# Normalisation moved back to VectorE in the output tiles, half a head moved into the chunk loop, and an early load dropped

## The chip, the cores and the metric

One Trainium2 chip, all 8 cores. Each core runs the same program on its own batch element; no core talks to another. The metric is device time in microseconds of the slowest core.

## The reference, cut to what matters

Per core, `x` is 2048 x 2048 float32 (`L` rows of `C` features). One layer joins a state-space branch `s` and a feed-forward branch `g`, both fed by the same layer-normed `xn`:

```python
xn = layernorm(x)                                  # mean m1, 1/std r1 per row
# s: a second layer norm, in_proj (C -> 96), conv of width 3, silu,
#    selective scan over 16 states -> y, then y @ out_proj_W.T + xn
s  = attn_ref(xn, ...)
# g: int8-like rows times ternary weights, w1, w3: 2048 -> 5632, w2: 5632 -> 2048
h  = silu(bitlinear(xn, w1)) * bitlinear(xn, w3)
g  = silu(bitlinear(h, w2))
return x + s * g
```

## The kernel before, in words

The program is a row of blocks. Inside a block each engine has its own in-order queue and they meet at semaphores; a block ends when all engines have ended it. Every `@blk.vector`, `@blk.scalar`, ... function appends to one engine's queue, so the order in which the Python code emits them is the order in which each engine runs them.

**`ph01`** (lines 380 to 702) works through `NE = 8` row blocks of 256 rows. For block `e`:

- `emit_xdma(e)` loads the rows into `xh2[e % 2]` from SP's queue. It waits until block `e - 2` has left the buffer.
- `emit_head(e)` (line 399): ScalarE computes mean and variance (L408 to L423, all small and large passes over the 2 row tiles); VectorE waits for them and normalises in place (L434, L437 x2), takes the row maximum (L444 x2) and makes the quantisation scales (L449 to L464). Then the scales are turned into a row and spread over the partitions: TensorE transposes (L474), VectorE copies (L483), SP sends two small transfers (L492), TensorE multiplies by ones (L500, L502), VectorE copies to `sxB` and `sxinvB` (L509, L511).
- `emit_chunks(e)` (line 516): ScalarE computes the statistics of the second norm (L525 to L540) once the head's scales are there. Then 16 chunks `cc`: TensorE transposes 128 columns (L562), VectorE copies them out (L574), TensorE multiplies them with the in-projection (L593), VectorE scales and casts them into `qx` (L583, L585).
- `emit_tail(e)` (line 602) spreads the second norm's factors in the same way (L613 to L671) and writes `xin` (L678 to L683).

The driver emits head(0), and then for each `e`: tail(e - 1), chunks(e), xdma(e + 2), head(e + 1), and from `e = 2` on two units of weight means (`emit_means`, POOL loads 1 MB, ScalarE sums it, L278).

**`attn`** (line 731) does the convolution and the scan. POOL builds a selection matrix `sel` (L734, L737) while VectorE makes two small operations for `nm1r1 = -m1 * r1` (L746, L748) and then starts the convolution (L750, L758, L762).

**`m13`** does the two big products with `w1` and `w3` and stores `h` to `h_scr` in device memory. **`hfin`** (line 1196) finds the row maxima of `h` and spreads the scales into `shB`. At its start POOL already loads the first two 512 KB tiles of `h` (L1202, `h_preload`).

**`m2_0` and `m2_1`** (line 1315) each compute half of the rows of `g`'s last product, in 11 slabs of 4 tiles `ht`. `emit_prep_early` loads `h` (L1360, POOL, each load waits for VectorE's product of two tiles earlier) and, in half 0, `w2T` (L1379, SP, 1 MB each, three buffers); VectorE scales `h` to integers (L1411), ScalarE copies to bfloat16 (L1429) and makes signs of the weights (L1448, L1451), VectorE adds them (L1475). `emit_m2_units` runs the matmuls (L1532) and VectorE adds each result to `f_half` (L1549, L1551).

Each half ends with 8 **output tiles** `tt` (lines 1573 to 1654), one per 128 rows:

- SP loads the tile of `x` (L1582), 1 MB, into `xre`. The load of tile `tt` is emitted behind the store of tile `tt - 1`, in one queue.
- TensorE computes `y @ out_proj` (L1601), four products of 512 columns, in turn into `ps_op` and the two `ps_f`, so each of them is free again two tiles later.
- ScalarE makes `silu` of `f_half` (L1612), and then normalises `xre` into `xnb` with `scale = r1`, `bias = nm1r1` (L1620).
- VectorE adds the product (L1632, or L1635 and L1638 as two halves), multiplies with the gate (L1641) and adds `xre` (L1643), and SP stores (L1651).

```python
sy.wait_ge(s_v.h, ob_hist.get(tt - 2, fwait[2 * tt + 1]))      # x load of tile tt, L1581
...
t.wait_ge(s_v.h, ob_hist[tt - 2])                              # matmul of tile tt, L1591
```

`ob_hist[tt]` is the semaphore value after L1643 of tile `tt`.

Of the kernel before, what the change touches and what calls it, by code (L numbers as in the profile page):

```python
# [15 lines left out]
C = 2048  # L16
# [31 lines left out]
def build_core_program(stop_after=None):  # L48
# [331 lines left out]
    with nc.Block("ph01") as blk:  # L380
# [18 lines left out]
        def emit_head(e):  # L399
# [68 lines left out]

            @blk.tensor
            def _(t):  # L470
                t.wait_ge(s_v.h, p4v_hist[e])
                if e >= 2:
                    t.wait_ge(s_v.h, bc2c_hist[e - 2])
                s_t.inc(t.transpose(ps_bc[0][0:2 * TPE, 0:128],  # L474
                                    xcol[:, sb1:sb1 + 2 * TPE], ident[:]))
# [40 lines left out]
        def emit_chunks(e):  # L516
# [31 lines left out]
            for cc in range(NCC):  # L548
                par = (2, 3, 0, 1)[cc % 4]
# [141 lines left out]
        emit_head(0)  # L691
        for e in range(NE):
            if e >= 1:
                emit_tail(e - 1)
            emit_chunks(e)
            if e + 2 < NE:
                emit_xdma(e + 2)
            if e + 1 < NE:
                emit_head(e + 1)
# [31 lines left out]
    with nc.Block("attn") as blk:  # L731
# [9 lines left out]
        nm1r1 = xcol[:, 3 * NTT:4 * NTT]  # L741
# [452 lines left out]
    h_preload = {}  # L1194

    with nc.Block("hfin") as blk:
        @blk.gpsimd
        def _(g):
# [110 lines left out]
    sgs_all = {}  # L1309
    hq_last = {0: None, 1: None}  # L1310
    prev_store = [0, 0]
    for half in range(2):
        hq_sems = {}
        hm1_sems = {}
        with nc.Block(f"m2_{half}") as blk:
# [6 lines left out]
            def emit_prep_early(sbi):  # L1322
# [24 lines left out]
                def _(g):  # L1347
                    for k in range(sbn):
                        ht = base + k
                        par = ht % 2  # L1350
                        if half == 0 and ht < 2:
                            hlds[k] = h_preload[ht]
                            continue
# [13 lines left out]
                if half == 0:  # L1367
                    for k in range(sbn):
                        sgs_all[base + k] = s_a.v + min(2, sbn) + k + 1
# [67 lines left out]
                if half == 0:  # L1437
# [3 lines left out]
                    def _(sc):  # L1441
                        for k in range(sbn):
# [13 lines left out]
                            assert sgs_all[ht] == got  # L1456
# [116 lines left out]
            for tt in range(TPH):  # L1573
# [14 lines left out]
                def _(t):  # L1588
                    t.wait_ge(s_v.h, fwait[2 * tt + 1])
                    if tt >= 2:  # L1590
                        t.wait_ge(s_v.h, ob_hist[tt - 2])  # L1591
                    if tt == 1:
                        t.wait_ge(s_v.h, f_ok)
                    inst = None
                    for j in range(4):
                        if tt % 2 == 0:
                            dst = ps_op[:, j * 512:(j + 1) * 512]
                        else:
                            dst = ps_f[j // 2][:, (j % 2) * 512:
                                               (j % 2 + 1) * 512]  # L1600
                        inst = t.matmul(dst,  # L1601
# [7 lines left out]
                def _(sc):  # L1609
                    sc.wait_ge(s_v.h, fwait[2 * tt + 1])  # L1610
                    sc.wait_ge(s_o[fp].h, st_hist.get(tt - 2, prev_store[fp]))
                    sc.activation(gbuf[:],  # L1612
                                  f_half[:, tt * C:(tt + 1) * C],
                                  AF.Silu, scale=hscol[:, gt:gt + 1])
                    sc.drain()
# [11 lines left out]
                def _(v):  # L1627
                    xnb = fscr1 if tt % 2 == 0 else sxinvB
                    v.wait_ge(s_t.h, opd)
                    v.wait_ge(s_a.h, gok)  # L1630
                    if tt % 2 == 0:
                        v.tensor_tensor(xnb[:], ps_op[:], xnb[:], ALU.add)  # L1632
                        v.drain()
                    else:
# [84 lines left out]
```

## Time and profile before

| | us |
|---|---|
| two timed runs | 3564.94 and 3662.07, median 3613.51 |
| profiled execution, its own time | 3567.97 |
| its span, slowest core (core 4) | 3566.3 |
| spans of the 8 cores | 3553.2 to 3566.3 |
| mean granted TensorE clock | 0.86 on every core |

The span runs from the first to the last instruction of core 4. Times of single instructions below are microseconds from its start. The profiled execution's own time is 1.7 us above its span; all terms below are set against that execution.

### The profile page before, as it was taken

To read this page: it belongs to the slowest core of one execution; us is meant where nothing else is said; L and a number is where in the kernel's file an instruction comes from. 1 tells how busy PE (TensorE), PEld (TensorE's weight loads), DVE (VectorE), ACT (ScalarE), POOL (GpSimd) and SP (SyncE) were. 2 spreads that over 40 slices of the span, in tenths; PEclk is the share of its full clock that TensorE was granted. 3 is DMA by queue.
4 is the path that set the end of the run, shared out by engine and by line. 5 is a ranking of instruction groups with operands and counts; after the bars stand their busy time and mean duration, and the time that the engine had idled before them with its cause. 6 is when DMAs were issued, how large, how long until landed. Compare 5 with 4: busy or idle time off the path is not lost. (4 is left out here: it accounts for less than half of the span.)

```text
span 3566.3 us, 29311 instructions; the slowest of 8 cores (3553.2 to 3566.3 us)
## 1 busy us (share of the span) xinstructions
PE 2501.6 (70%) x9525; PEld 1088.6 (31%) x9525; DVE 1844.2 (52%) x1799; ACT 1684.5 (47%) x1360; POOL 151.2 (4%) x283
## 2 busy tenths in 40 slices
PE   2454454996999999999999994355656733766772
PEld 1222221332444444444444442122222311323331
DVE  2545444884445554455445445445555534656653
ACT  3252514886666666666666661554453232111122
POOL 0000001110000000000000000000000000000000
PEclk9999996556999999999999996677778866888885
DMA  3112103996445454445454541554454234232213
GB/s 112 47 67 75 48 0 118 335 308 234 140 140 143 142 143 140 140 142 143 141 142 142 142 118 36 188 177 153 130 189 134 85 123 141 100 125 106 84 62 127
DMA packets 92611, 469.14 MB, mean 132 GB/s; under 512 B 12924, under 2 KB 13004, under 8 KB 58060
## 3 DMA queue, kind: packets, MB, share of 16 engines
q1 hardware_dynamic: 54412, 282.69, 25.1%
q0 software_dynamic: 38048, 184.57, 16.6%
q8 instruction: 78, 1.28, 0.2%
q14 instruction: 73, 0.60, 0.1%
HBM read 381.20 MB, written 85.98 MB: 131 GB/s over the span
## 5 line engine op out<-in xcount | busy, mean ns | idle before, releaser
L1532 PE MATMUL ps_f<-w2s,qhs 128*128 128x512 bf16 x2816 | 680.0, 407 | 425.4 <-DVE f_half L1551 261.9
L1071 PE MATMUL ps_a<-qx,w1q 128*128 128x512 bf16 x2816 | 632.2, 383 | 85.6 <-DVE hbuf L1116 73.7
L1079 PE MATMUL ps_b<-qx,w3q 128*128 128x512 bf16 x2816 | 622.1, 379 | 0.0
L1532 PEld LDWEIGHTS ps_f<-w2s,qhs 128*128 128x128 bf16 x2816 | 288.8, 103 | 818.0 <-issue 589.4
L1551 DVE TENSOR_TENSOR f_half<-f_half,ps_f 128x1024 f32<-128x1024 f32 x320 | 390.9, 1221 | 195.9 <-PE ps_f L1532 190.1
L1071 PEld LDWEIGHTS ps_a<-qx,w1q 128*128 128x128 bf16 x2816 | 275.1, 99 | 434.7 <-issue 118.5
L1079 PEld LDWEIGHTS ps_b<-qx,w3q 128*128 128x128 bf16 x2816 | 275.6, 98 | 332.2
L1429 ACT ACT_TABLE_LOAD x44 | 56.5, 1283 | 573.1 <-DVE fscr L1411 571.8
L1104 ACT ACT_TABLE_LOAD x88 | 112.9, 1283 | 447.5 <-DVE fscr L1095 447.5
L1411 DVE TENSOR_TENSOR fscr<-hbuf,shB 128x1024 int32<-128x1024 f32 x88 | 107.8, 1225 | 252.4 <-DMA hbuf<-h_scr 235.7
L1112 DVE TENSOR_TENSOR fscr<-ps_b,sxinvB 128x1024 f32<-128x1024 f32 x88 | 107.8, 1225 | 230.9 <-ACT fscr L1104 230.9
L593 PE MATMUL ps_ip<-xnTc,inprojT_sb 128*96 128x256 f32 x256 | 145.8, 672 | 107.9 <-DVE xnTc L574 107.9
L1042 DVE TENSOR_TENSOR w1q<-gscr 128x2048 bf16<-128x2048 bf16 x44 | 53.9, 1225 | 248.0 <-ACT gscr L1022 248.0
L1095 DVE TENSOR_TENSOR fscr<-ps_a,sxinvB 128x1024 f32<-128x1024 f32 x88 | 107.8, 1225 | 41.7 <-PE ps_b L1079 14.5
L887 PE MATMUL ps_sc<-bp_sb,sel 16*96 16x512 f32 x128 | 112.5, 1057 | 22.6 <-DVE y_sb L855 22.6
L525 ACT ACT_TABLE_LOAD x8 | 10.3, 1283 | 249.3 <-DVE xcol L464 249.3
L1051 DVE TENSOR_TENSOR w3q<-gscr 128x2048 bf16<-128x2048 bf16 x44 | 53.9, 1225 | 131.4 <-ACT gscr L1031 131.4
L1163 ACT ACT_TABLE_LOAD x88 | 112.9, 1283 | 11.4 <-issue 1.2
L1116 DVE SCALAR_TENSOR_TENSOR hbuf<-fscr,thrall 128x1024 f32<-128x1024 f32 x88 | 113.1, 1285 | 6.5
L574 DVE COPY xnTc<-ps_tr 128x256 f32<-128x256 f32 x128 | 54.4, 425 | 118.3 <-PE ps_tr L562 117.1
L908 PE MATMUL ps_cc<-cp_sb,sel 16*96 16x512 f32 x128 | 112.5, 1056 | 0.0
L1135 DVE SCALAR_TENSOR_TENSOR fscr<-hbuf 128x1024 f32<-128x1024 f32 x88 | 107.9, 1226 | 8.9 <-issue 0.2
(206 smaller groups left out, 2816.0 us busy)
## 6 DMA issues: line engine op xcount, KB each, us to landing
wstg<-w1L SPq DMA_DIRECT2D x44, 1024.0 KB, 11.6
wstg<-w3L SPq DMA_DIRECT2D x44, 1024.0 KB, 14.0
w2m<-w2T SPq DMA_DIRECT2D x88, 512.0 KB, 6.3
h_scr<-hbuf POOLq DMA_DIRECT2D x88, 512.0 KB, 4.2
hbuf<-h_scr POOLq DMA_DIRECT2D x88, 512.0 KB, 7.1
wstg<-w2T SPq DMA_DIRECT2D x30, 1024.0 KB, 9.4
wstg<-w1L POOLq DMA_DIRECT2D x22, 1024.0 KB, 7.6
wmst<-w1L POOLq DMA_DIRECT2D x22, 1024.0 KB, 9.6
```

The source lines that it names most:

```text
L593: inst = t.matmul(ps_ip[:], inprojT_sb[:, cc * D:(cc + 1) * D], xsl, start=(cc == 0), stop=(cc == NCC - 1))
L887: inst = t.matmul(ps_sc[0:D, j * 512:(j + 1) * 512], sel[:, n * D:(n + 1) * D], bp_sb[:, j * 512:(j + 1) * 512], start=True, stop=True)
L908: inst = t.matmul(ps_cc[0:D, j * 512:(j + 1) * 512], sel[:, n * D:(n + 1) * D], cp_sb[:, j * 512:(j + 1) * 512], start=True, stop=True)
L1071: t.matmul(ps_a[pu][:, j * 512:(j + 1) * 512], w1q[par][:, cc * 128:(cc + 1) * 128], qx[:, cc * L + th * HALF + j * 512: cc * L + th * HAL ...
L1079: inst = t.matmul(ps_b[pu][:, j * 512:(j + 1) * 512], w3q[par][:, cc * 128:(cc + 1) * 128], qx[:, cc * L + th * HALF + j * 512: cc * L + t ...
L1095: s_v.inc(v.tensor_tensor(fscr1[:, 0:HALF], ps_a[pu][:], sxinvB[:, th * HALF:(th + 1) * HALF], ALU.mult))
L1104: s_a.inc(sc.activation(fscr2[:, 0:HALF], fscr1[:, 0:HALF], AF.Silu, scale=thrall[:, 2:3]))
L1116: s_v.inc(v.scalar_tensor_tensor(hbuf[pu][:], fscr1[:, 0:HALF], thrall[:, 5:6], fscr2[:, 0:HALF], ALU.mult, ALU.mult))
L1135: v.scalar_tensor_tensor(fscr1[:, 0:HALF], hbuf[pu][:], -1.0, hbuf[pu][:], ALU.mult, ALU.max)
L1163: s_a.inc(sc.activation(w2m[wpar][:], w2m[wpar][:], AF.Abs, accum_out=mtmp[:, (2 + hf) * NH + ht: (2 + hf) * NH + ht + 1]))
L1532: inst = t.matmul(ps_f[pu][:, j * 512:(j + 1) * 512], qhs[sp][:, k * HALF + tt * 128: k * HALF + (tt + 1) * 128], w2s[sp][:, k * C + ch * ...
L1551: s_v.inc(v.tensor_tensor(dst, dst, ps_f[pu][:], ALU.add))
```

## The change

Three independent edits.

1. In `ph01` the head is cut in two. `emit_head_a` holds the load wait, ScalarE's statistics, and VectorE's normalisation up to the scales (L434 to L464). `emit_head_b` holds the transposition and spreading. `emit_chunks` gets a callback which emits `head_a(e + 1)` ahead of chunk 10 of block `e`; `head_b(e + 1)` stays where the head was.
2. In the output tiles the normalisation of `x` goes from ScalarE (L1620) to a `tensor_scalar` on VectorE, `nm1r1` and its two operations (L746, L748) go, and all tiles use `ps_op`, so that the matmuls of tile `tt` wait for VectorE's last operation of tile `tt - 1` instead of `tt - 2`.
3. The early load of the first two tiles of `h` (L1202) goes; they are loaded by `emit_prep_early` like the others.

```diff
-        def emit_head(e):
+        def emit_head_a(e):
...
             p4v_hist[e] = s_v.v
 
+        def emit_head_b(e):
+            sb1 = 3 * NTT + (e % 2) * 8
+
             @blk.tensor
...
-        def emit_chunks(e):
+        def emit_chunks(e, mid_cb=None):
...
             for cc in range(NCC):
+                if cc == 10 and mid_cb is not None:
+                    mid_cb()
...
         for e in range(NE):
             if e >= 1:
                 emit_tail(e - 1)
-            emit_chunks(e)
+            cb = (lambda e=e: emit_head_a(e + 1)) if e + 1 < NE else None
+            emit_chunks(e, cb)
             if e + 2 < NE:
                 emit_xdma(e + 2)
             if e + 1 < NE:
-                emit_head(e + 1)
+                emit_head_b(e + 1)
...
-            v.tensor_tensor(nm1r1, m1c[:], r1c[:], ALU.mult)
-            v.drain()
-            v.tensor_single_scalar(nm1r1, nm1r1, -1.0, ALU.mult)
-            v.drain()
...
-            for ht in range(2):
-                par = ht % 2
-                g.wait_ge(s_hd[par].h, hstore_total[par])
-                s_hd[par].inc(g.dma_start(
-                    out=hbuf[par][:],
-                    in_=dr["h_scr"][ht * 128:(ht + 1) * 128, 0:HALF]), 16)
-                h_preload[ht] = s_hd[par].v
...
                     t.wait_ge(s_v.h, fwait[2 * tt + 1])
-                    if tt >= 2:
-                        t.wait_ge(s_v.h, ob_hist[tt - 2])
-                    if tt == 1:
-                        t.wait_ge(s_v.h, f_ok)
+                    if tt >= 1:
+                        t.wait_ge(s_v.h, ob_hist[tt - 1])
...
-                    xnb = fscr1 if tt % 2 == 0 else sxinvB
-                    sc.wait_ge(s_x.h, xld)
-                    if tt >= 2:
-                        sc.wait_ge(s_v.h, ob_hist[tt - 2])
-                    s_a.inc(sc.activation(xnb[:], xre[:], AF.Identity,
-                                          scale=r1c[:, gt:gt + 1],
-                                          bias=nm1r1[:, gt:gt + 1]))
...
+                    v.wait_ge(s_x.h, xld)
                     v.wait_ge(s_t.h, opd)
                     v.wait_ge(s_a.h, gok)
...
+                    v.tensor_scalar(fscr1[:], xre[:], m1c[:, gt:gt + 1],
+                                    r1c[:, gt:gt + 1], ALU.subtract, ALU.mult)
+                    v.drain()
+                    v.tensor_tensor(fscr1[:], ps_op[:], fscr1[:], ALU.add)
+                    v.drain()
+                    v.tensor_tensor(fscr2[:], fscr1[:], gbuf[:], ALU.mult)
```

VectorE's queue before, from the end of chunk 15 of a block into the head of the next:

```order
L585 CAST qx<-fscr 128x256
L429 UNCONDITIONAL_BRANCH
L434 RECIPROCAL r1c<-sq 128x2
L437 TENSOR_SCALAR xh_0<-xh_0,m1c,r1c 128x2048 x2
L444 TENSOR_REDUCE stat<-xh_0 128x1 x2
...
L464 COPY xcol<-xcol 128x2
L478 UNCONDITIONAL_BRANCH
L483 COPY rowbuf<-ps_bc 4x128
```

The same engine after the change, from the end of chunk 9 on (lines shifted by 5: L590 is the old L585, L579 the old L574, L486 the old L483):

```order
L590 CAST qx<-fscr 128x256
L429 UNCONDITIONAL_BRANCH
L434 RECIPROCAL r1c<-sq 128x2
L437 TENSOR_SCALAR xh_0<-xh_0,m1c,r1c 128x2048 x2
L444 TENSOR_REDUCE stat<-xh_0 128x1 x2
...
L464 COPY xcol<-xcol 128x2
L574 UNCONDITIONAL_BRANCH
L579 COPY xnTc<-ps_tr 128x256
...
L590 CAST qx<-fscr 128x256
L481 UNCONDITIONAL_BRANCH
L486 COPY rowbuf<-ps_bc 4x128
```

The normalisation now stands between chunks 9 and 10, and the copy of the transposed scales follows chunk 15 directly. ScalarE's queue keeps its order.

VectorE's queue in two output tiles before:

```order
L1632 TENSOR_TENSOR fscr<-ps_op,fscr 128x2048
L1641 TENSOR_TENSOR fscr<-fscr,wstg 128x2048
L1643 TENSOR_TENSOR wstg<-fscr,wstg 128x2048
L1626 UNCONDITIONAL_BRANCH
L1635 TENSOR_TENSOR sxinvB<-ps_f,sxinvB 128x1024
L1638 TENSOR_TENSOR sxinvB<-ps_f,sxinvB 128x1024
L1641 TENSOR_TENSOR fscr<-sxinvB,wstg 128x2048
L1643 TENSOR_TENSOR wstg<-fscr,wstg 128x2048
```

and in one output tile after (every tile is alike):

```order
L1597 TENSOR_SCALAR fscr<-wstg,m1c,r1c 128x2048
L1600 TENSOR_TENSOR fscr<-ps_op,fscr 128x2048
L1602 TENSOR_TENSOR fscr<-fscr,wstg 128x2048
L1604 TENSOR_TENSOR wstg<-fscr,wstg 128x2048
```

One operation has come to VectorE, and the two half additions of the odd tiles have become one.

## Rows read from the trace of the kernel before

**Rows 1.** The page, part 1: busy time, share of the span, instructions.

```profile
PE 2501.6 (70%) x9525; PEld 1088.6 (31%) x9525; DVE 1844.2 (52%) x1799; ACT 1684.5 (47%) x1360; POOL 151.2 (4%) x283
```

**Rows 2.** Busy time by stretch: m2_0's slabs, its output tiles, m2_1's output tiles.

```profile
2227.00:2841.00 614.00, 358.02 (x1418) 149.33 (x1419) 323.34 (x265) 273.64 (x170) 22.18 (x42) 0.76 0.47 151
2841.00:2967.00 126.00, 39.97 (x55) 15.25 (x53) 55.17 (x28) 34.36 (x19) 0.00 (x0) 0.60 0.33 117
...
3436.00:3566.00 130.00, 39.21 (x54) 14.66 (x52) 54.85 (x28) 34.36 (x19) 0.00 (x0) 0.61 0.34 121
```

**Rows 3.** Timeline of ph01: start, duration, engine, line, operation, idle before.

```profile
250.25 0.42 DVE L574 COPY xnTc<-ps_tr 128x256 f32<-128x256 f32 x1 [0.16 <-issue]
...
255.63 0.39 ACT L423 ACTIVATE sq<-ssum,cns 128x2 f32<-128x2 f32 x1
...
284.71 0.42 DVE L574 COPY xnTc<-ps_tr 128x256 f32<-128x256 f32 x1 [1.00 <-PE ps_tr L562]
...
285.72 0.29 DVE L585 CAST qx<-fscr 128x256 bf16<-128x256 int32 x1
286.25 0.17 DVE L434 RECIPROCAL r1c<-sq 128x2 f32<-128x2 f32 x1 [0.23 <-issue]
...
295.27 0.17 DVE L464 COPY xcol<-xcol 128x2 f32<-128x2 f32 x1
...
296.24 0.28 DVE L483 COPY rowbuf<-ps_bc 4x128 f32<-4x128 f32 x1 [0.80 <-PE ps_bc L474]
```

**Rows 4.** Timeline of the start of attn.

```profile
539.87 1.48 POOL L734 IOTA sel<- 16x1536 f32 x1 [154.84 <-SPq L731]
...
540.21 1.17 DVE L748 TENSOR_SCALAR xcol<-xcol 128x16 f32<-128x16 f32 x1
541.46 5.22 DVE L750 TENSOR_SCALAR ucv<-xin,convw_sb,convb_sb 96x2048 f32<-96x2048 f32 x1
541.51 4.09 POOL L737 TENSOR_SCALAR sel<-sel 16x1536 f32<-16x1536 f32 x1 [0.17 <-issue]
```

**Rows 5.** Timeline of the output tiles of m2_0, and two rows of m2_1's.

```profile
2862.17 2.29 DVE L1643 TENSOR_TENSOR wstg<-fscr,wstg 128x2048 f32<-128x2048 f32 x1
...
2864.96 0.39 SPq L1582 DMA_DIRECT2D wstg<-x  x1
...
2871.99 2.09 ACT L1620 ACTIVATE fscr<-wstg,xcol,r1c 128x2048 f32<-128x2048 f32 x1 [11.42 <-DMA wstg<-x]
2874.19 2.29 DVE L1632 TENSOR_TENSOR fscr<-ps_op,fscr 128x2048 f32<-128x2048 f32 x1 [9.73 <-ACT fscr L1620]
...
2878.92 2.29 DVE L1643 TENSOR_TENSOR wstg<-fscr,wstg 128x2048 f32<-128x2048 f32 x1
...
2895.94 2.29 DVE L1643 TENSOR_TENSOR wstg<-fscr,wstg 128x2048 f32<-128x2048 f32 x1
...
3528.51 6.93 PE L1601 MATMUL ps_f<-outprojT_sb,y_sb 96*128 96x512 f32 x8 [10.08 <-DVE wstg L1643]
```

**Rows 6.** The line L437 in all of the trace: count, ns min/median/max.

```profile
L437 DVE TENSOR_SCALAR xh<-xh,m1c,r1c x16: 1345/1346/1348, 51.6 to 471.3; 128x2048 f32<-128x2048 f32 x16
```

**Rows 7.** Timeline of the start of m2_0.

```profile
2227.28 1.23 DVE L1411 TENSOR_TENSOR fscr<-hbuf,shB 128x1024 int32<-128x1024 f32 x1 [0.52 <-PEq L1196]
...
2241.47 1.22 DVE L1411 TENSOR_TENSOR fscr<-hbuf,shB 128x1024 int32<-128x1024 f32 x1 [11.58 <-DMA hbuf<-h_scr]
...
2245.36 1.23 DVE L1411 TENSOR_TENSOR fscr<-hbuf,shB 128x1024 int32<-128x1024 f32 x1 [2.67 <-DMA hbuf<-h_scr]
...
2256.92 2.00 ACT L1448 ACTIVATE wstg<-wstg,thrall 128x2048 bf16<-128x2048 f32 x1 [4.78 <-DMA wstg<-w2T]
...
2264.80 5.54 PE L1532 MATMUL ps_f<-w2s,qhs 128*128 128x512 bf16 x16 [40.44 <-DVE fscr L1411]
```

**Rows 8.** Timeline of the start of m2_1.

```profile
2967.32 1.04 POOL L1360 DMA_DIRECT2D hbuf<-h_scr  x2 [211.59 <-POOLq L1315]
...
2983.28 1.22 DVE L1411 TENSOR_TENSOR fscr<-hbuf,shB 128x1024 int32<-128x1024 f32 x1 [3.96 <-DMA hbuf<-h_scr]
```

More of the change, by code:

```diff
@@ L690, in build_core_program @@
         emit_xdma(1)
-        emit_head(0)
+        emit_head_a(0)
+        emit_head_b(0)
         for e in range(NE):
@@ L739, in build_core_program @@
         sel_ok = s_g.v
-        nm1r1 = xcol[:, 3 * NTT:4 * NTT]
         @blk.vector
@@ L1192, in build_core_program @@
     ps_f = [PS4(f"ps_f{i}", (128, HALF)) for i in range(2)]
-    h_preload = {}
     with nc.Block("hfin") as blk:
-        @blk.gpsimd
-        def _(g):
-            for ht in range(2):
-                par = ht % 2
-                g.wait_ge(s_hd[par].h, hstore_total[par])
-                s_hd[par].inc(g.dma_start(
-                    out=hbuf[par][:],
-                    in_=dr["h_scr"][ht * 128:(ht + 1) * 128, 0:HALF]), 16)
-                h_preload[ht] = s_hd[par].v
         thrw2 = finalize_mean(blk, (2 * NH, 4 * NH), 6, ps_op,
@@ L1308, in build_core_program @@
     wq_sems = {}
-    sgs_all = {}
     hq_last = {0: None, 1: None}
@@ L1350, in _ @@
                         par = ht % 2
-                        if half == 0 and ht < 2:
-                            hlds[k] = h_preload[ht]
-                            continue
                         if ht >= 2:
@@ L1365, in _ @@
                         hlds[k] = s_hd[par].v
-                if half == 0:
-                    for k in range(sbn):
-                        sgs_all[base + k] = s_a.v + min(2, sbn) + k + 1
                 wlds = {}
@@ L1455, in _ @@
                             sgs[k] = got
-                            assert sgs_all[ht] == got
                 if sbn > 2:
@@ L1589, in _ @@
                     t.wait_ge(s_v.h, fwait[2 * tt + 1])
-                    if tt >= 2:
-                        t.wait_ge(s_v.h, ob_hist[tt - 2])
-                    if tt == 1:
-                        t.wait_ge(s_v.h, f_ok)
+                    if tt >= 1:
+                        t.wait_ge(s_v.h, ob_hist[tt - 1])
                     inst = None
                     for j in range(4):
[L1596 to L1601, printed above, removed]
+                        inst = t.matmul(ps_op[:, j * 512:(j + 1) * 512],
                                         y_sb[:, gt * 128:(gt + 1) * 128],
@@ L1611, in _ @@
                     sc.wait_ge(s_o[fp].h, st_hist.get(tt - 2, prev_store[fp]))
[L1612 to L1615, printed above, removed]
-                    xnb = fscr1 if tt % 2 == 0 else sxinvB
-                    sc.wait_ge(s_x.h, xld)
-                    if tt >= 2:
-                        sc.wait_ge(s_v.h, ob_hist[tt - 2])
-                    s_a.inc(sc.activation(xnb[:], xre[:], AF.Identity,
-                                          scale=r1c[:, gt:gt + 1],
-                                          bias=nm1r1[:, gt:gt + 1]))
+                    s_a.inc(sc.activation(gbuf[:],
+                                          f_half[:, tt * C:(tt + 1) * C],
+                                          AF.Silu, scale=hscol[:, gt:gt + 1]))
                     sc.drain()
@@ L1627, in _ @@
                 def _(v):
-                    xnb = fscr1 if tt % 2 == 0 else sxinvB
+                    v.wait_ge(s_x.h, xld)
                     v.wait_ge(s_t.h, opd)
                     v.wait_ge(s_a.h, gok)
[L1631 to L1634, printed above, removed]
-                        v.tensor_tensor(xnb[:, 0:1024], ps_f[0][:],
-                                        xnb[:, 0:1024], ALU.add)
-                        v.drain()
-                        v.tensor_tensor(xnb[:, 1024:2048], ps_f[1][:],
-                                        xnb[:, 1024:2048], ALU.add)
-                        v.drain()
-                    v.tensor_tensor(fscr2[:], xnb[:], gbuf[:], ALU.mult)
+                    v.tensor_scalar(fscr1[:], xre[:], m1c[:, gt:gt + 1],
[4 more added lines that the diff above has]
+                    v.tensor_tensor(fscr2[:], fscr1[:], gbuf[:], ALU.mult)
                     v.drain()
```

## The prediction

> **What bounds the kernel now.** I read the page first: TensorE is busy for 70% of the span, VectorE for 52%, ScalarE for 47% [rows 1]. No engine is the bound of the whole, so each edit has to be priced in its own stage. Next I read the stretches. In the output tiles of either half TensorE is busy for 40 of 126 us and 39 of 130, VectorE for 55, ScalarE for 34, and the DMA engines at a third [rows 2]: nothing is full there, it is a chain. In the slabs of the first half no engine is full either (358, 323 and 274 of 614 us) [rows 2]. Then I followed the timeline at each of the four places that the diff touches. The large products of m13 (two thirds of TensorE's work) are not touched, nor is anything that they wait for.
>
> The chain of one output tile: VectorE's last operation of tile tt-1 ends at 2864.46 (2862.17 plus 2.29). SP issues the store and then the x load, at 2864.96. ScalarE has idled for 11.42 us when the load lets it start at 2871.99, 7.53 us after 2864.46. VectorE waits for ScalarE and starts at 2874.19, and three operations later it ends at 2881.21 (2878.92 plus 2.29) [rows 5]. So an even tile takes 16.75 us: 7.53 for store issue and load, 2.20 for ScalarE's pass with its handover, 7.02 for VectorE. The next, odd tile ends at 2898.23 (2895.94 plus 2.29), 17.02 us later, since its addition comes in two halves [rows 5]. TensorE is not in this chain, although it too starts only when VectorE has ended.
>
> **Edit 2, output tiles.** ScalarE's pass (2.20 us with the handover) leaves the chain. In its place VectorE runs a TENSOR_SCALAR over 128 x 2048 float32 with two per-row numbers. That is the very shape of L437: 1.346 us, in all 16 cases within 2 ns [rows 6]; with a gap of 0.07, as between VectorE's other neighbours, 1.42. A tile takes 7.53 + 1.42 + 7.02 = 15.97 us. Even tiles save 0.78, odd ones 1.05. Per half, tiles 1, 3, 5, 7 save 4.2 and tiles 2, 4, 6 save 2.3. Tile 0 loses: its x was there long before, ScalarE's pass was done beside the slabs, and now 1.42 us stand behind the last matmul. Net 5.1 per half, **-10.2 us** for both.
>
> The added wait: TensorE now begins tile tt after VectorE's end of tile tt-1. Before, at that same moment it began tile tt+1. So the start of its work is where it was, and only its consumer comes sooner. The slowest of these groups of 8 matmuls took 6.93 us [rows 5]; the granted clock was 0.60 to 0.61 in these stretches [rows 2], so much of it ran at 1.2 GHz. From VectorE's end to TensorE's end are then about 0.05 + 6.93 = 7.0 us, with a handover of 0.2 it is 7.2, and the load needs 7.53. The load stays last, by 0.3 us. Cost nothing; if this cover goes, each microsecond that TensorE is late costs 14 us over the 14 tiles. Silu stays on ScalarE, has no load ahead of it any more and runs far ahead of VectorE. Nothing else is queued behind TensorE's wait.
>
> **Edit 2, start of attn.** The small operations L746 and L748 stood ahead of the convolution. L748 handles 16 columns and yet took 1.17 us: it began while POOL's IOTA ran and ended at 541.38, when IOTA ended (541.35). L750 took 5.22 us and ended at 546.68, about a microsecond behind POOL's L737 (541.51 plus 4.09 is 545.60) [rows 4]. I read this as VectorE standing still while POOL works. Without the two, L750 is the one that stands waiting when IOTA ends, as L748 did, and gets its turn in the 0.16 us gap before L737: it would end at 541.35 + 1.35 = 542.7, or **-4.0 us**. The other end is 0: L737 comes first and L750 ends at 546.7 as before. I take -4.0, since L748 shows that the waiting operation goes first.
>
> The Trainium skill says in its GPSIMD Engine Reference, section Specifications, that GpSimd's access to SBUF is shared with VectorE, with contention against VectorE's two-port operations. These rows agree with it. By that page L1597 meets no such contention in the output tiles, where POOL has no row.
>
> **Edit 1, the head.** A chunk has VectorE idle for 1.00 us before its copy L574, in every chunk. Before, from the end of chunk 15 (285.72 plus 0.29, 286.01) to L483 at 296.24 there were 10.23 us: 0.24 gap, 9.19 for L434 to L464, 0.80 for TensorE's transposition [rows 3]. After, the 9.19 stand between chunks 9 and 10. There TensorE has finished chunk 10's transposition long before, so that L574 follows with a 0.16 gap, as the first chunk of a block does at 250.25 [rows 3]: 0.24 + 9.19 + 0.16 in place of the 1.00. At the end the scales' transposition has nothing to wait for, and L483 follows after some 1.00. Sum 8.59 + 1.00 = 9.59 against 10.23: 0.64 saved per head, seven heads, **-4.5 us**. VectorE and TensorE take turns in the chunks, so the 9.19 us themselves are not hidden: they stop the chunks wherever they stand. Bounds: 0, and 0.80 + 0.24 of each head saved, 7.3. ScalarE's statistics for the moved part end at 256.02 in the block whose first copy is at 250.25 and whose chunk 10 comes ten chunks of some 2.3 us later (three VectorE operations of 1.3 us in all and the 1.00 idle), at 273 [rows 3]; they are there in time by 17 us. The x load behind them and SP's queue keep their places, and ScalarE's second statistics start earlier, which nobody waits for.
>
> **Edit 3, the early load.** Before, VectorE scaled the first two tiles of h at once (2227.28), and the fourth at 2245.36, 18.1 us into the block, with 4 MB asked of the DMA engines till then (two tiles of h and three of w2T) [rows 7]. Behind the fourth product stand the first weight sum and thereby a weight load, the signs that wait for it (2256.92) and the first matmul (2264.80) [rows 7]. Without the early load the same engines have 5 MB to move before the fourth product. In proportion that is 22.6 us in place of 18.1, **+4.5 us**. The other bound is from the second half, which starts cold: the second product began 16.0 us after the first issue [rows 8], here it began 1.4 us into the block, so at most +14.6. The lower bound is 0, should the weight loads be what the signs wait for. I take 4.5, from the nearest rows. The slabs behind are a chain too [rows 2], so I carry the delay through undiminished.
>
> The Trainium skill has in DMA: Bandwidth & Descriptors, section Queues, rings and completion order, that each DMA engine serves the queues it has work for in turn, packet by packet. By that the h loads would not stand behind three weight loads but take half the rate, and the sum would be that of the rival "hidden" below. The trace speaks against it: the third tile's load kept VectorE waiting 11.58 us [rows 7].
>
> **Sum.** -10.2 - 4.0 - 4.5 + 4.5 = -14.2 us. From the profiled execution's 3567.97 us that gives 3553.8, rounded 3554. The two timed runs are 3564.94 and 3662.07; the profiled execution agrees with the lower one, and the median of 3613.51 is only the mean of two unlike runs.
>
> **The rivals.**
>
> - *Given back.* The first two h loads cost their full 14.6 us, and L750 loses its turn to L737: -10.2 - 4.5 + 14.6 = -0.1, 3568 us. For it: the second half's start [rows 8]. Against it: there 4 MB of w2s stood beside the h loads, here 3.
> - *Hidden.* The h loads share the engines evenly with the weight loads and are off the chain: -18.7, 3549 us. Against it: the 11.58 us.
> - *VectorE's added operation is slow.* A TENSOR_SCALAR took 5.22 us once [rows 4]. If the 16 new ones did, each would cost 3.87 more than counted, 62 us: 3553.8 + 62 = 3616 us, slower than before. It decides from 2.24 us per operation on (14.2 / 16 = 0.89 above 1.35). Against it: POOL has no work in the output tiles [rows 2], and L437 never took more than 1.348.
> - *The moved head waits in the middle.* If ScalarE's statistics came late, VectorE would stop at chunk 9 with TensorE behind it. Their passes take some 11 us, seven heads: 77 us, 3631 us. Against it: the 17 us of slack.
> - *TensorE becomes last in the output tiles.* If its work ended 1 us later than I have it, 0.7 x 14 = 10 us go: 3564.
>
> **How the numbers follow.** Chances: forecast 0.60 (3554, own range 3544 to 3565), given back 0.17, hidden 0.09, TensorE last 0.07, slow operation 0.03, late head 0.01, and 0.03 for what I do not see. The range reaches from 3540 (the hidden case with edit 1 at its bound is 3546, less some noise) to 3616, the slow operation: the upper side is wide because one run of the same kernel lay 97 us above the other. A measurement of this kernel can tell about 2% (71 us) from no change. No case reaches -71 us; the late head and half of the unseen would be at +2%. Faster 0.02, same 0.95, slower 0.03.
>
> **What would show it.** In the output tiles: VectorE idle before the new operation about 7.5 us, released by the x load and not by TensorE; 1.35 us each; tiles 16.0 us apart. In ph01: 9.4 us without chunks between chunks 9 and 10, no wait for ScalarE there, each block 0.6 us shorter. In attn: L750's duration and the end of POOL's L737. In m2_0: the first matmul some 42 us after the block's start instead of 37.5. The prediction is wrong if the stretches in between (m13, the slabs) change their lengths, or if the added operation takes other than 1.35 us.

## The result and the profile after

| | before | after |
|---|---|---|
| median of the runs, us | 3577.54 (3564.94 to 3727.86, 32 runs) | 3598.38 (3582.9 to 3768.95, 33 runs) |
| ratio after to before, 95% interval | | 1.005 (1.0033 to 1.0067) |
| profiled execution, its own time, us | 3567.97 | 3592.93 |
| its span on the slowest core, us | 3566.3 | 3591.3 |
| granted clock of its cores | 0.860 to 0.864 | 0.859 to 0.867 |

Some executions of either kernel run at a lower granted clock on some of the cores and take up to 5% longer; the ratio compares the others. The changed kernel is slower by 0.5%, some 18 us (0.005 x 3577.54). That is inside the 2% of "no change" and inside the range, but the forecast was 14 us faster, and the interval excludes every gain: the sign of the sum was wrong. Part 1 of the page after, which answers to [rows 1]:

```profile
PE 2503.7 (70%) x9525; PEld 1090.1 (30%) x9525; DVE 1862.5 (52%) x1805; ACT 1651.6 (46%) x1344; POOL 152.0 (4%) x283
```

The page sees that work moved from ScalarE to VectorE (18 us more on DVE, 33 less on ACT) and little else. Where the time went is in the stages. For the table the same marks (the first and last instruction of a stage) were read on all 8 cores of a profiled execution; it gives the medians over the cores, in us. The row "tiles 1 to 7" runs from the start of VectorE's last operation of tile 0 to the first load of half 1 (some 3 us behind the last tile's), the row below it from there to the start of VectorE's last operation of the last tile. The last column is explained with the experiments.

| stage | before | after | difference | forecast | after, x load behind the tail |
|---|---|---|---|---|---|
| ph01: first L434 to POOL's IOTA | 488.5 | 512.1 | **+23.6** | -4.5 | 482.9 |
| start of attn: IOTA to the end of the convolution | 11.8 | 10.2 | -1.6 | -4.0 | 10.2 |
| scan | 293.1 | 292.8 | -0.3 | 0 | 292.3 |
| m13 | 1340.1 | 1338.0 | -2.1 | 0 | 1337.3 |
| end of m13 to the block m2_0 | 43.6 | 43.5 | -0.1 | 0 | 43.5 |
| m2_0, start to first matmul | 35.6 | 40.8 | +5.2 | +4.5 | 41.2 |
| slabs, to VectorE's last operation of tile 0 | 579.3 | 582.8 | +3.5 | +1.4 | 583.9 |
| tiles 1 to 7 of half 0 | 123.4 | 118.0 | -5.4 | -6.5 | 118.0 |
| from there to the end of half 1 | 591.2 | 585.6 | -5.6 | -5.1 | 587.2 |
| sum | | | **+17.2** | -14.2 | |

The sum of the differences is what the ratio says (+18). All stages but one came within 3 us of the forecast; ph01 missed by 28.

What TensorE waits for in ph01 and the start of attn, in the kernel after (the time waited in all, how often, the longest, in us):

```profile
PE ps_bc L503 <- DMA rows<-rowbuf: 53.5, 8, 8.8
...
PE ps_bc L664 <- DMA rows<-rowbuf: 22.5, 8, 2.9
```

And the same two lines of code in the kernel before:

```profile
PE ps_bc L500 <- DMA rows<-rowbuf: 22.6, 8, 2.9
PE ps_bc L659 <- DMA rows<-rowbuf: 22.5, 8, 2.9
```

`rows` is the pair of 1 KB transfers with which the head spreads the scales over the partitions. The tail's pair (L664, before L659) costs 2.8 us each time, before and after. The head's pair cost 2.8 each time before, and now costs 53.5 in all. Two of the eight heads have no x load near them; the other six take (53.5 - 2 x 2.8) / 6 = 8.0 us each. The timeline of one of them, after (start, duration, engine, line, operation, idle before with its releaser):

```profile
243.30 0.37 SPq L387 DMA_DIRECT2D xh<-x  x1
243.55 0.28 DVE L486 COPY rowbuf<-ps_bc 4x128 f32<-4x128 f32 x1 [0.79 <-PE ps_bc L477]
243.90 1.25 SPq L495 DMA_DIRECT2D rows<-rowbuf  x2
...
251.19 1.19 PE L503 MATMUL ps_bc<-rows,ones 1*128 1x256 f32 x2 [7.82 <-DMA rows<-rowbuf]
251.25 1.28 ACT L408 ACT_TABLE_LOAD   x1 [10.81 <-DMA xh<-x]
253.34 0.43 DVE L512 COPY sxB<-ps_bc 128x256 f32<-128x256 f32 x1 [9.51 <-PE ps_bc L505]
```

and one of the kernel before:

```profile
286.56 0.37 SPq L387 DMA_DIRECT2D xh<-x  x1
...
296.59 1.17 SPq L492 DMA_DIRECT2D rows<-rowbuf  x2
...
298.90 1.19 PE L500 MATMUL ps_bc<-rows,ones 1*128 1x256 f32 x2 [2.84 <-DMA rows<-rowbuf]
```

Before, SP issues the 2 MB x load at 286.56 and the small rows 10.0 us later; they land in 2.3 (296.59 to 298.90). After, SP issues the rows 0.6 us behind the load, and they land 7.3 us later, at 251.19, in the same moment as the load (ScalarE, which waits for it, goes on at 251.25). Over the six blocks and eight cores it is 6.9 to 8.4 us, 7.1 in the median. The 9.2 us of VectorE's work that edit 1 moves away were what had stood between the two. VectorE shows the price on L512: 9.51 us idle. The copy L486, on which the forecast's saving rested, does come 0.79 us after the last chunk.

### The profile page after: what moved, and what is told of

The parts are those of the page before. It is cut to its first block and busy times, and to the rows that moved or that the text cites. A ratio compares the mean times of both kernels' runs of the same rounds, so it can differ in the third digit from the quotient of the medians.

```text
span 3591.3 us, 29279 instructions; the slowest of 8 cores (3573.8 to 3591.3 us)
## 1 busy us (share of the span) xinstructions
PE 2503.7 (70%) x9525; PEld 1090.1 (30%) x9525; DVE 1862.5 (52%) x1805; ACT 1651.6 (46%) x1344; POOL 152.0 (4%) x283
## 5 line engine op out<-in xcount | busy, mean ns | idle before, releaser
L1575 PE MATMUL ps_op<-outprojT_sb,y_sb 96*128 96x512 f32 x128 | 96.1, 921 | 137.9 <-DVE wstg L1604 137.9
L888 PE MATMUL ps_sc<-bp_sb,sel 16*96 16x512 f32 x128 | 112.5, 1057 | 22.6 <-DVE y_sb L856 22.6
L598 PEld LDWEIGHTS ps_ip<-xnTc,inprojT_sb 128*96 128x96 f32 x256 | 50.6, 259 | 216.2 <-issue 216.2
L579 DVE COPY xnTc<-ps_tr 128x256 f32<-128x256 f32 x128 | 54.4, 425 | 113.5 <-PE ps_tr L567 110.6
```

Source lines behind the costliest of these rows:

```text
L598: inst = t.matmul(ps_ip[:], inprojT_sb[:, cc * D:(cc + 1) * D], xsl, start=(cc == 0), stop=(cc == NCC - 1))
L888: inst = t.matmul(ps_sc[0:D, j * 512:(j + 1) * 512], sel[:, n * D:(n + 1) * D], bp_sb[:, j * 512:(j + 1) * 512], start=True, stop=True)
```

## The experiments

The first theory: edit 1 lets the row transfers run into the x load. Rivals: another edit lengthens ph01; the order in SP's queue is at fault (theory Q), against the 16 DMA engines being full whichever queue is used (theory E); or the head in the middle costs the time by itself (theory S).

**Edit 1 alone.** The kernel before with `emit_head` cut in two and the callback ahead of chunk 10:

```diff
-            emit_chunks(e)
+            cb = (lambda e=e: emit_head_a(e + 1)) if e + 1 < NE else None
+            emit_chunks(e, cb)
...
-                emit_head(e + 1)
+                emit_head_b(e + 1)
```

> The kernel before with edit 1 alone (the head cut in two, its first part ahead of chunk 10). Theory Q: the two small row transfers of head_b now follow the 2 MB load of x by 0.6 us in SP's queue instead of 10 us, and land only when it has (about 7.3 us instead of 2.3), in the 6 blocks that have such a load: ph01 ends 24 us later than before, total +22 to +25. Rival M: ph01 is not the cause, the added time lies in edits 2 and 3: then ph01 ends 4.5 us earlier and the total is -4.

Measured: ratio 1.0066 (1.002 to 1.0111); ph01 512.3 us, +23.8; the other stages as before, but for the slabs (561.1, with cores between 548 and 581). The longest wait for the rows, on core 2:

```profile
112.15 0.38 SPq L387 DMA_DIRECT2D xh<-x  x1
112.74 1.98 SPq L495 DMA_DIRECT2D rows<-rowbuf  x2
...
121.01 1.19 PE L503 MATMUL ps_bc<-rows,ones 1*128 1x256 f32 x2 [8.80 <-DMA rows<-rowbuf]
```

The whole loss of ph01 is edit 1.

**The rows on another queue.** Edit 1 alone, and the head's row transfers are issued by POOL:

```diff
-            @blk.sync
+            @blk.gpsimd
...
-                    s_ld.inc(sy.dma_start(
+                    s_rp.inc(sy.dma_start(
```

> Edit 1 alone, but head_b's two row transfers are issued by POOL instead of SP, with a semaphore of their own. Theory Q (they stand in line behind the x load in SP's queue): in POOL's queue nothing is ahead, they land within about 3 us, ph01 ends some 4 us earlier than before, total -4. Rival E (the x load keeps the 16 DMA engines full, whichever queue the rows are in): they still land after some 7 us, ph01 ends 20 us or more later than before, total +20.

Measured: ratio 0.9987 (0.9949 to 1.0024), which tells nothing; ph01 515.9 us (+27.4) does. The timeline of core 2 (POOL's row is the issue of the rows):

```profile
109.65 0.37 SPq L388 DMA_DIRECT2D xh<-x  x1
110.70 1.03 POOL L496 DMA_DIRECT2D rows<-rowbuf  x2 [50.31 <-DVE rowbuf L487]
...
117.53 1.19 PE L504 MATMUL ps_bc<-rows,ones 1*128 1x256 f32 x2 [7.82 <-DMA rows<-rowbuf]
118.38 1.28 ACT L409 ACT_TABLE_LOAD   x1 [11.60 <-DMA xh<-x]
```

The rows leave through POOL's queue 1.05 us behind the load and land 6.8 us later, 0.85 ahead of it. So the other queue is no remedy, and theory E's number came: while the 2 MB are moved, two small transfers wait in either queue. (Without an x load ahead, in the last head, POOL's take 2.2 to 3.2 us.) But theory Q doesn't fall with it for SP's own queue. The trace also records what the DMA engines moved, in packets; the load has 256 large ones. The first line below is edit 1 alone, core 7, 112.00 to 119.20 us; the other two are the rows through POOL's queue, core 7, 109.00 to 116.90 us (queue q1 is SP's, q0 POOL's; packets, MB):

```profile
DMA packets 248, 2.03 MB, mean 282 GB/s; under 512 B 0, under 2 KB 0, under 8 KB 0
...
q1 hardware_dynamic: 243, 1.99, 64.3%
q0 software_dynamic: 64, 0.00, 0.5%
```

In SP's queue none of the rows (packets of 512 B) has moved when 248 of the load's 256 packets have; in all six blocks and on all cores at most 3 of the load's packets come after them. They move in the order of the queue. Through POOL's queue they overtake the load's last 32 to 77 packets, and are still late: their first packet moves 3.7 to 5.7 us after the issue. The Trainium skill says in DMA: Bandwidth & Descriptors, section Queues, rings and completion order, that each DMA engine serves the queues it has work for in turn; that the rows of another queue are through at once does not follow, as the timeline shows. The sharing goes the other way too: in the last block POOL issues two weight loads of 1 MB right behind the head's rows, and the tail's rows, issued by SP 7.4 us later, take 5.6 to 6.2 us instead of 2.3. That is one reason why ph01 is a little longer here than with SP.

**The load behind the rows.** Edit 1 alone, `emit_xdma(e + 2)` emitted after `emit_head_b(e + 1)` instead of before it:

```diff
-            if e + 2 < NE:
-                emit_xdma(e + 2)
             if e + 1 < NE:
                 emit_head_b(e + 1)
+            if e + 2 < NE:
+                emit_xdma(e + 2)
```

> Edit 1 alone, but the load of x for block e+2 is emitted behind head_b(e+1), so that the row transfers are ahead of it in SP's queue. Theories Q and E: head_b's rows land in 2.3 us again; the tail's rows, now some 7 us behind the x load, may lose up to 2 us per block; ph01 ends between 4.5 us earlier and 8 us later than before. Rival S (the stop in the middle of the chunks costs the time itself): ph01 ends 24 us later as with edit 1.

Measured: ph01 483.0 us, 5.5 less than before the change and 29.3 less than with edit 1 alone; ratio 0.9992 (0.9965 to 1.0018).

```profile
229.58 1.17 SPq L495 DMA_DIRECT2D rows<-rowbuf  x2
230.90 0.37 SPq L387 DMA_DIRECT2D xh<-x  x1
231.88 1.19 PE L503 MATMUL ps_bc<-rows,ones 1*128 1x256 f32 x2 [2.83 <-DMA rows<-rowbuf]
```

The rows take 2.3 us again. The head in the middle costs nothing by itself (S falls); it brings 5.5 us, once the load is out of the rows' way. The tail's rows, which SP issues 6.2 to 6.4 us behind the load, take 2.3 us as before.

**The load behind the tail's rows as well:**

```diff
                 emit_tail(e - 1)
+                if e + 1 < NE:
+                    emit_xdma(e + 1)
...
-            if e + 2 < NE:
-                emit_xdma(e + 2)
```

> Edit 1 alone, with the load of x emitted behind the tail of the block, so that both pairs of row transfers are ahead of it. Theories Q and E: all rows land in 2.3 us, ph01 ends 4.5 us earlier than before (0.64 us for each of seven heads), total -4. If the x load comes too late for the statistics ahead of chunk 10, VectorE waits for ScalarE there and the gain shrinks. Rival S: +24.

Measured: ph01 482.9 us, the same as above; ratio 0.9983 (0.9957 to 1.0008).

**Half of the load ahead.** To see whether the wait goes with the bytes in flight: edit 1 alone, x in two transfers of 1 MB, one ahead of the rows and one behind them.

```diff
-                emit_xdma(e + 2)
+                emit_xdma(e + 2, 0)
...
                 emit_head_b(e + 1)
+            if e + 2 < NE:
+                emit_xdma(e + 2, 1)
```

> Edit 1 alone, with the 2 MB load of x cut into two transfers of 1 MB, the first ahead of head_b's rows and the second behind them. If the rows wait for the bytes in flight ahead of them, they now land about 4.5 us after their issue instead of 7.3, or 2.3 without a load: ph01 some 13 us less long than with edit 1, that is 8 to 12 us longer than before's. Rival: the wait is a fixed cost of following any load: ph01 stays 24 us longer; or the second half takes the engines as well: 20 us or more.

Measured: ph01 497.6 us, +9.1 against before; ratio 1.0039 (1.0009 to 1.0069). On core 2:

```profile
239.12 0.33 SPq L388 DMA_DIRECT2D xh<-x  x1
239.73 1.17 SPq L496 DMA_DIRECT2D rows<-rowbuf  x2
241.05 0.33 SPq L388 DMA_DIRECT2D xh<-x  x1
...
245.17 1.19 PE L504 MATMUL ps_bc<-rows,ones 1*128 1x256 f32 x2 [5.96 <-DMA rows<-rowbuf]
```

From issue to the matmul, medians over blocks and cores: 2.3 us with nothing ahead, 4.7 with 1 MB (4.3 to 6.0; the one shown took 5.4), 7.1 with 2 MB (7.0 to 8.4). ph01: 483.0, 497.6, 512.3: half the bytes ahead, half the loss. The second 1 MB, issued 1.3 us behind the rows, doesn't hold them: by the packet records 102 of its 128 packets or more move after them. So it is the bytes ahead in the queue that count.

**Edit 2 alone** (the output tiles and the start of attn as in the diff of the change):

> The kernel before with edit 2 alone (normalisation on VectorE in the output tiles, one product buffer, nm1r1 gone). By the prediction's step: tiles 16.0 us apart instead of 16.9, tile 0 longer by 1.4, per half -5.1; the start of attn 1.6 us shorter (as the trace of the changed kernel has it, not 4.0). Total -12 us. Rival: TensorE's single buffer makes it last in the tiles (tiles 16.9 us or more apart): total 0 or more.

Measured: ratio 0.999 (0.9959 to 1.0021). Tiles 1 to 7 of half 0 take 117.9 us (-5.5), half 1 587.1 (-4.1), the start of attn 10.1 (-1.7), and m13 1337.9 (-2.2), where nothing was expected. The start of attn on its slowest core:

```profile
539.06 2.47 DVE L744 TENSOR_SCALAR ucv<-xin,convw_sb,convb_sb 96x2048 f32<-96x2048 f32 x1 [0.46 <-PEq L380]
541.69 5.06 DVE L752 SCALAR_TENSOR_TENSOR ucv<-xin,convw_sb,ucv 96x2047 f32<-96x2047 f32 x1 [0.16 <-DVE ucv L744]
546.82 2.35 DVE L756 SCALAR_TENSOR_TENSOR ucv<-xin,convw_sb,ucv 96x2047 f32<-96x2047 f32 x1
```

The first operation (L750 before) does go first, in 2.47 us instead of 5.22. But POOL's work is still there, and now the second operation stands in it: 5.06 where its twin takes 2.35.

**Edit 3 alone** (the early load dropped):

> The kernel before with edit 3 alone (no early load of h). By the prediction's step the first matmul of m2_0 comes 4.5 us later after the block's start, as the changed kernel has it (+5.2 in the median of its cores), and all other stretches stay: total +5 us. Rival: later slabs have slack that takes the delay back, total 0. The 2 us that m13 is shorter in the changed kernel would show here if the missing early load were their cause.

Measured: the first matmul 41.2 us into the block, +5.6; ratio 1.0032 (0.9993 to 1.0071); m13 as before, so the 2.2 us of m13 are not from edit 3.

**POOL's two operations behind the convolution.** The kernel before, with the iota and the comparison that make `sel` moved in POOL's queue to wait for the convolution, to test whether VectorE stands still while POOL works:

```diff
+            g.wait_ge(s_v.h, cvd)
             g.iota(sel[:], [[1, NST], [0, D]], channel_multiplier=-1,
```

> The kernel before, with POOL's two operations that build sel (L734, L737) moved behind the convolution of attn; nothing left out. If VectorE stood still there because POOL worked (the prediction's reading), L748 takes some 0.17 us and L750 1.3 us instead of 1.17 and 5.22, and the convolution ends 5 us earlier: total -5 us. Rival: the 5.22 us belong to L750 itself (its shape, 96 partitions): unchanged, total 0.

Measured: from the first L434 to the end of the convolution 495.5 us against 500.3, -4.8; ratio 0.9986 (0.9965 to 1.0007). The same two operations as in [rows 4]:

```profile
539.67 0.17 DVE L739 TENSOR_SCALAR xcol<-xcol 128x16 f32<-128x16 f32 x1
539.92 1.34 DVE L741 TENSOR_SCALAR ucv<-xin,convw_sb,convb_sb 96x2048 f32<-96x2048 f32 x1
```

0.17 us in place of 1.17, and 1.34 in place of 5.22, with POOL's two operations out of the way: VectorE had stood still for them.

**The x load ahead of the store in the output tiles.** The kernel before, with the load of x for tile `tt + 1` issued ahead of the store of tile `tt` in SP's queue instead of behind it (and a semaphore for each of the two buffers). It asks what the chain of a tile is worth without the 7.5 us of load in it:

```diff
-                @blk.sync
-                def _(sy):
-                    sy.wait_ge(s_v.h, ob_hist.get(tt - 2, fwait[2 * tt + 1]))
...
-                xld = s_x.v
+                if tt == 0:
+                    emit_xld(0)
+                if tt + 1 < TPH:
+                    emit_xld(tt + 1)
+                xld = xlds[tt]
```

> The kernel before, with the load of x for output tile tt+1 put ahead of the store of tile tt in SP's queue (two semaphores for the two buffers), so that it runs during the tile before. The chain of one tile then has no load: VectorE's 7.1 us, TensorE's 6.9 us in parallel (two product buffers), 2 MB of transfers that took some 7.5 us. Tiles some 8 us apart instead of 16.9: 14 x 8.5 = 120 us less, total 3450 us. Rival: the transfers share the engines so that store and load together are the bound at 12 us or more a tile: -60 us.

Measured: ratio 0.9723 (0.9657 to 0.9788), some 99 us, from two executions only. Tiles 1 to 7 of half 0: 66.4 us instead of 123.4; half 1: 541.8 instead of 591.2. By the stages -106, where -120 was expected. What is last now:

```profile
2857.50 2.29 DVE L1644 TENSOR_TENSOR fscr<-ps_op,fscr 128x2048 f32<-128x2048 f32 x1 [3.36 <-ACT fscr L1632]
...
2859.11 1.28 ACT L1624 ACT_TABLE_LOAD   x1 [1.71 <-DMA out<-wstg]
```

In the even tiles VectorE waits for ScalarE (3.4 us here, 3.8 in the mean of six), which itself waits for the store that frees its buffer. The order of two entries in one queue was worth more than all that the change does.

**The same in the changed kernel:**

> The changed kernel with the load of x for output tile tt+1 put ahead of the store of tile tt. The load is then no longer last, and what the prediction called hidden is bare: TensorE starts only at VectorE's end of the tile before and takes 7.0 us, then VectorE 8.4. Tiles 15.5 us apart, against 16.0 with the load in the chain and 8 to 9 with two product buffers: only some 7 us less than the changed kernel. Rival: TensorE at the higher clock, 3.6 us: 12 us a tile, 55 us less.

Measured: ratio 1.0038 (1.0019 to 1.0058); tiles 1 to 7 of half 0 111.0 us instead of 118.0, half 1 578.8 instead of 585.6: -13.8, and not -106. The reason stands in the timeline of its output tiles:

```profile
2904.81 7.08 PE L1587 MATMUL ps_op<-outprojT_sb,y_sb 96*128 96x512 f32 x8 [8.77 <-DVE wstg L1616]
2912.44 1.35 DVE L1609 TENSOR_SCALAR fscr<-wstg,m1c,r1c 128x2048 f32<-128x2048 f32 x1 [7.78 <-PE ps_op L1587]
```

VectorE waits for TensorE (in all 16 tiles of core 7), and TensorE for VectorE's last operation of the tile before: all tiles now share `ps_op`. Before the change the odd tiles used `ps_f`, and the two engines overlapped. That wait of edit 2 costs nothing in the changed kernel, because the load is as long. In kernels whose loads are in time, these two stretches are 82 us longer with edit 2 than without (111.0 - 66.4 and 578.8 - 541.8). VectorE's added operation has its part in that, by an estimate up to 16 x 1.42 = 23 us; no run has the one without the other, so the price of the single buffer by itself is not shown.

**The changed kernel with the x load of ph01 behind the tail:**

> The changed kernel with one line moved: the load of x is emitted behind the tail, so that both pairs of row transfers are ahead of it. If the x load ahead of head_b's rows is all that makes the changed kernel slower, ph01 is 5.6 us shorter than before's instead of 24 longer, everything else as in the changed kernel: 29 us less than the changed kernel, about 12 us less than before, ratio to before 0.997. Rival: some other cost of the combination of the edits remains, ratio 1.000 or more.

Measured: ratio 0.9985 (0.9959 to 1.0011); ph01 482.9 us, all other stages as in the changed kernel (last column of the table above). With one load moved, ph01 is 29.2 us shorter, and the rest of the change stands as it was. By the stages that is 12 us less than before the change; the interval of the ratio doesn't tell it from no change.

**The best of it.** The kernel before with edit 1 and the x load behind the tail, POOL's `sel` behind the convolution, and the early x load; without edits 2 and 3:

> The kernel before (two product buffers, normalisation on ScalarE, early load of h) with three things: edit 1 with the load of x behind the tail (-5.6), sel built behind the convolution (-4.8), the x load of the output tiles one tile ahead (-106). Together -116 us, ratio 0.967 to 0.970. Rival: the gains overlap or slow the cores of a die against each other: -100 or less.

Measured: median 3457.57 us (3450.13 to 3562.44, 6 runs), ratio 0.9659 (0.964 to 0.9679): 122 us faster than before by the ratio (0.0341 x 3577.54). ph01 and the convolution take 489.7 us (before 500.3), tiles 1 to 7 of half 0 66.1, half 1 537.6. Busy time in its output tiles of half 0 (core 7), columns as in [rows 2]:

```profile
2831.00:2897.00 66.00, 34.68 (x57) 13.03 (x55) 51.28 (x27) 32.28 (x18) 0.00 (x0) 0.72 0.57 207
```

VectorE is busy for 51.3 of 66 us, 78%, where it was 55 of 126 in [rows 2], and the DMA engines for 57% of the time instead of 33%: the same work, with VectorE now near to being the bound of a tile.

## Why the prediction was wrong in its sign

**Edit 1: the step that failed** is "The x load behind them and SP's queue keep their places". In the order of SP's queue this is true, and it is what the listing of the change showed. In time it is not. The 9.2 us of VectorE's work had stood between the issue of the x load and that of the rows (10.0 us apart), and the load was over when the rows came. Moved away, the two are 0.6 us apart. The prediction followed what the moved work waits for and who waits for it, and not what its duration had kept apart; it put the rows' wait for the load at nothing, without a term. The term comes out as +23.6: -5.6 for the moved head (measured with the load out of the way; forecast -4.5, with 7.3 as its bound), and +29 for six row transfers of 4.8 us more each (7.1 instead of 2.3). Shown by five kernels: edit 1 alone, the load behind the rows and behind the tail, half of it ahead, and the changed kernel with the load moved. No rival had it. The late head (77 us) spoke of ScalarE's statistics, which were in time as forecast.

**Edit 2, output tiles:** forecast -10.2, measured -5.4 in tiles 1 to 7 of half 0 and -5.6 in half 1; with the 1.4 forecast for tile 0 of half 0, which the noise of the slabs hides, that makes -9.6. The mechanism is right. The rows of the new operation over all of the trace (count and ns, then VectorE's idle time ahead of it by releaser), and two tiles after the change, on core 1:

```profile
L1597 DVE TENSOR_SCALAR fscr<-wstg,m1c,r1c x16: 1345/1346/1347, 2868.0 to 3578.6; 128x2048 f32<-128x2048 f32 x16
...
  DMA wstg<-x: 86.1, 11
  ACT wstg L1586: 17.8, 2
  PE ps_op L1575: 12.0, 3
```

```profile
2874.12 2.29 DVE L1604 TENSOR_TENSOR wstg<-fscr,wstg 128x2048 f32<-128x2048 f32 x1
2876.56 6.90 PE L1575 MATMUL ps_op<-outprojT_sb,y_sb 96*128 96x512 f32 x8 [8.77 <-DVE wstg L1604]
2883.87 1.35 DVE L1597 TENSOR_SCALAR fscr<-wstg,m1c,r1c 128x2048 f32<-128x2048 f32 x1 [7.45 <-DMA wstg<-x]
...
2890.02 2.29 DVE L1604 TENSOR_TENSOR wstg<-fscr,wstg 128x2048 f32<-128x2048 f32 x1
2906.33 2.29 DVE L1604 TENSOR_TENSOR wstg<-fscr,wstg 128x2048 f32<-128x2048 f32 x1
```

The new operation takes 1.346 us in all 16 cases, as [rows 6] promised: the rival "slow operation" falls, and with it the upper end of the range, which it had set. VectorE idles 7.45 us, released by the load (forecast 7.5); the two tiles are 15.90 and 16.31 us long (forecast 15.97). TensorE ends at 2883.46 (2876.56 plus 6.90), and the operation begins 0.41 later: the cover was 0.3 to 0.4 us, as thin as worked out, and it held. Of the three waits put down to TensorE, two are tile 0 of a half, behind the slabs (2.29 us each), and the third is 7.45 long, like those of the load. In the two put down to ScalarE, the Silu that ended last is that of the next tile, which this wait doesn't need; the load's last packet had ended 0.5 to 0.6 us before the operation, as in most tiles that are put down to the load.

What the forecast had not is tiles of up to 17.97 us on this core. In each of its four tiles over 16.5 us, a packet of an engine's instructions stands among those of store and load, and one of the 16 DMA engines ends the load 0.9 to 1.8 us behind the others. From the DMA queues between 2925.00 and 2935.00, in the longest of these tiles (queue, kind: packets, MB):

```profile
q14 instruction: 1, 0.01, 0.5%
```

Over the eight cores, 73 of the 112 tiles have no such packet and take 15.9 to 16.7 us; the 39 with one take up to 18.1. Before the change it was 89 without (16.6 to 17.8) and 23 with one (up to 18.8). A tile without became 0.81 us shorter in the mean (16.87 to 16.06; forecast 0.93), and more tiles have one after the change. That the packet is the cause goes by this count; no experiment moved it.

**Edit 2, start of attn:** forecast -4.0, measured -1.6. The reading of the rows was right (sel_later: -4.8, 5.22 down to 1.34), the conclusion was not. I had the waiting operation get its turn and forgot that POOL's remaining 4 us then meet the next one:

```profile
564.53 1.48 POOL L741 IOTA sel<- 16x1536 f32 x1 [165.67 <-SPq L738]
564.63 2.46 DVE L751 TENSOR_SCALAR ucv<-xin,convw_sb,convb_sb 96x2048 f32<-96x2048 f32 x1 [0.46 <-PEq L380]
566.18 4.86 POOL L744 TENSOR_SCALAR sel<-sel 16x1536 f32<-16x1536 f32 x1 [0.17 <-issue]
567.25 5.06 DVE L759 SCALAR_TENSOR_TENSOR ucv<-xin,convw_sb,ucv 96x2047 f32<-96x2047 f32 x1 [0.16 <-DVE ucv L751]
```

Here the wait went only when POOL's work went.

**Edit 3:** forecast +4.5, measured +5.2 (+5.6 alone). The start of m2_0 after, beside [rows 7]:

```profile
2248.06 0.80 SPq L1361 DMA_DIRECT2D wstg<-w2T  x2
...
2269.88 1.22 DVE L1393 TENSOR_TENSOR fscr<-hbuf,shB 128x1024 int32<-128x1024 f32 x1 [1.60 <-DMA hbuf<-h_scr]
...
2288.59 5.56 PE L1513 MATMUL ps_f<-w2s,qhs 128*128 128x512 bf16 x16 [43.27 <-DVE fscr L1393]
```

The fourth product stands 21.8 us into the block (2269.88 less 2248.06, where SP issues the first load of the block), where the share of bytes gave 22.6. The forecast "some 42 instead of 37.5" for the first matmul was read on one core, on which it came late (37.7 us from SP's first load; 34.8 to 38.1 over the cores); after the change the cores have 39.7 to 42.1. The rivals "given back" and "hidden" fall with it: the loads cost neither 14.6 nor nothing.

**The stages between** were named as a sign that the prediction is wrong if they move. m13 became 2.1 us shorter, with edit 2 alone as well, and not with edit 1 or 3. Where it comes from can be read. TensorE runs the product L1071 in 88 groups of 32 matmuls; most take 7.07 us, some 8.8. One near the end of m13 on core 0, before and with edit 2 alone:

```profile
2136.44 8.75 PE L1071 MATMUL ps_a<-qx,w1q 128*128 128x512 bf16 x32 [2.52 <-DVE hbuf L1116]
...
2133.26 7.07 PE L1065 MATMUL ps_a<-qx,w1q 128*128 128x512 bf16 x32 [2.16 <-DVE hbuf L1110]
```

The granted clock is 0.83 from 2135.00 to 2145.00 before, and 1.00 from 2133.00 to 2143.00 with edit 2. Before the change 5 to 8 of the 88 groups take over 7.6 us on each core, in the four kernels with edit 2 it is 2 to 6. Why edit 2, which touches nothing in m13, leaves TensorE fewer of them stays open. The slabs show +3.5 where 1.4 was expected. Their instructions are the same in all kernels here that keep edit 3 out, and yet they take 545 to 594 us, with 37 us between two cores of one execution (the load behind the rows); so these 2 us are not to be read as an effect.

## What to carry to other kernels

When a step is moved, list for each queue which two issues it had stood between, and how long the first of them is in flight: an unchanged order in a queue is not an unchanged distance in time. A transfer of 1 KB on which an engine waits belongs ahead of every bulk load, and another queue doesn't replace that (6.8 us instead of 7.3). Where a chain has a load in it, look first at whether the load could have been issued earlier: here that was worth 106 us by the stages, while the edits to the arithmetic around it were worth 10; and a buffer given up because its wait is hidden today is a price that the next improvement pays.

## What the runs showed of the hardware that was not expected

- Two transfers of 1 KB, from issue to the matmul that waits for them: 2.3 us alone, 4.3 to 6.0 with 1 MB issued ahead, 6.9 to 8.4 with 2 MB in the same queue, where they move behind all but a few of its 256 packets (10 at most); 5.8 to 8.1 (6.8 in the timeline) when they came through POOL's queue 1.05 us behind SP's 2 MB.
- VectorE stands still while POOL's IOTA or TENSOR_SCALAR runs, for two kinds of operation: TENSOR_SCALAR 1.34 to 5.22 us, and a SCALAR_TENSOR_TENSOR with two tensors 2.35 to 5.06. POOL's own time grew a little when VectorE had gone first (4.09 to 4.86).
- A load of 1 MB behind a store of 1 MB ends up to 2 us later in tiles in which one packet of an engine's instructions (8 or 16 KB) goes through one of the same 16 DMA engines (a count, no experiment): in the changed kernel tiles of up to 18.1 us, and of 16.7 at most without one.
- The stretch of slabs, the same instructions, differs between cores and executions by up to 49 us (545 to 594) at nearly the same mean clock of the cores' whole spans (0.865 and 0.857). This hid every difference of 10 us in the whole times, and so the stages, and not the ratios, carry most verdicts above.
